# Attention maxima of the second layer: the causal mask moved from VectorE's reduction to a TensorE product, and small pieces joined in pairs

## The reference, cut to what matters

```python
# 32 heads of 16, S = 1024
scores = einsum('bqhd,bkhd->bhqk', q, k) * scale
bias = slopes[:, None, None] * rel                # rel = key position - query position
causal = rel <= 0
scores = where(causal, scores + bias, -inf)
probs = softmax(scores, axis=-1)
attn = einsum('bhqk,bkhd->bqhd', probs, v)
```

## Time and profile before

| | us |
|---|---|
| median of 3 runs (lowest, highest) | 1939.48 (1938.72, 1940.89) |
| the profiled execution | 1937.06 |
| its span, first to last instruction | 1935.3 |
| TensorE (PE) busy in it | 1842.5 |
| VectorE (DVE) busy | 1137.5 |
| ScalarE (ACT) busy | 475.4 |
| GpSimd (POOL) busy | 986.4 |
| mean granted TensorE clock, share of full speed | 0.974 |

### The profile page before, as it was taken

One profiled execution on the slowest core, in us unless ns is written; L12 is line 12 of the kernel. 1 busy time (PEld: TensorE's weight loads), 2 busy tenths in 40 slices (PEclk: granted clock), 3 DMA queues, 4 the chain that ended last, 5 costly groups with the idle time before them and its releaser, 6 DMA issues. The chain is left out here.

```text
span 1935.3 us, 27511 instructions
## 1 busy us (share of the span) xinstructions
PE 1842.5 (95%) x10157; PEld 1445.1 (75%) x10157; DVE 1137.5 (59%) x1939; ACT 475.4 (25%) x623; POOL 986.4 (51%) x1148
## 2 busy tenths in 40 slices
PE   6999999999999999999999789998889999988998
PEld 5888888888888888888888568886654444357887
DVE  6674674874856747748747733304676888535601
ACT  4221111221211212112112120002414666633200
POOL 5676755755846657557535455444711121235432
PEclk9999999999999999999999899998987999899999
DMA  2111111111111111111101122202043333011112
GB/s 95 46 55 57 45 42 46 43 50 40 43 41 46 49 41 43 39 42 49 49 14 54 44 67 82 68 22 73 3 80 52 56 54 54 2 34 46 48 49 71
DMA packets 50501, 93.57 MB, mean 48 GB/s; under 512 B 8752, under 2 KB 13488, under 8 KB 50032
## 3 DMA queue, kind: packets, MB, share of 16 engines
q1 hardware_dynamic: 49776, 91.13, 17.3%
q10 hardware_dynamic: 640, 1.31, 0.4%
HBM read 76.15 MB, written 2.10 MB: 40 GB/s over the span
## 5 line engine op out<-in xcount | busy, mean ns | idle before, releaser
L366 POOL TENSOR_TENSOR a_w_l<-a_raw,a_w_h 128x1024 fp32r<-128x1024 f32 x96 | 205.6, 2141 | 8.0
L711 DVE TENSOR_TENSOR x<-x,a_ps 128x1024 f32<-128x1024 f32 x64 | 78.0, 1219 | 167.9 <-PE a_ps L165 167.9
L1596 ACT ACTIVATE a_pr<-a_ps 128x1024 f32<-128x1024 f32 (+1 forms) x192 | 153.3, 812 | 90.2 <-PE a_ps L1803 73.2
L1546 POOL TENSOR_SCALAR_AFFINE_SELECT a_pr<-a_pr 128x256 f32<-128x256 f32 x128 | 52.0, 406 | 217.0 <-ACT a_pr L1596 215.3
L1823 PE MATMUL a_ps<-a_K,a_Q 64*128 64x512 f32 (+2 forms) x384 | 136.5, 448 | 11.5 <-DVE a_mx L1702 8.8
L165 PE MATMUL a_ps<-a_tt_h,a_w_l 128*128 128x512 f32 x376 | 147.1, 391 | 0.0
L164 PE MATMUL a_ps<-a_tt_l,a_w_h 128*128 128x512 f32 x376 | 146.6, 390 | 0.0
L163 PE MATMUL a_ps<-a_tt_h,a_w_h 128*128 128x512 f32 x376 | 146.5, 390 | 0.0
L72 POOL TENSOR_TENSOR tick<-neg_half 128x1 f32<-128x1 f32 x120 | 35.0, 292 | 215.2 <-PE a_ps L165 208.1
L1698 DVE CUSTOM_DVE_ANT_0 a_masked<-a_ps,a_mask 128x384 bf16<-128x384 f32 (+3 forms) x256 | 115.0, 486 | 32.5 <-PE a_ps L1823 31.2
L1823 PEld LDWEIGHTS a_ps<-a_K,a_Q 64*128 64x128 f32 x384 | 66.7, 198 | 84.7 <-DVE a_mx L1702 33.4
(11 more groups left out here) (247 smaller groups left out, 4727.7 us busy)
## 6 DMA issues: line engine op xcount, KB each, us to landing
a_raw<-in_a_wpair SPq DMA_DIRECT2D x96, 256.0 KB, 2.7
f_raw<-in_f_w SPq DMA_DIRECT2D x33, 320.0 KB, 2.9
a_raw_s<-in_a_wout SPq DMA_DIRECT2D x32, 256.0 KB, 3.2
f_raw<-in_f_w SPq DMA_DIRECT2D x32, 256.0 KB, 2.6
a_raw_s<-in_a_wv SPq DMA_DIRECT2D x28, 256.0 KB, 2.6
a_cst<-in_a_cst SPq DMA_DIRECT2D x32, 129.0 KB
a_Q<-a_q_h SPq DMA_DIRECT2D x64, 64.0 KB
a_K<-a_k_h SPq DMA_DIRECT2D x54, 64.0 KB
```

Source lines behind the costliest of these rows:

```text
L366: nc.gpsimd.tensor_tensor(to_l, src, to_h, ALU.subtract).then_inc(s(done), 1)
L711: nc.vector.tensor_tensor(a, a, units[i], ALU.add).then_inc(s("out_added"), 1)
L1546: nc.gpsimd.affine_select(tri, tri, [[0, 2], [1, P]], ALU.is_ge, 0.0, base=0, channel_multiplier=-1).then_inc(s("selected"), 1)
L1596: nc.scalar.activation(pr[n % SLOTS][:, 2 * i:2 * i + 2, 0:width], S[at % 2][:, :, skip:skip + width], ACT.Exp, scale=0.25).then_inc(s("sc ...
```

## The change

Each diagonal piece now gets its mask from TensorE: right behind the product of a piece stands a second, bf16 product with `laterb` and `identb` into the 128 columns of its diagonal block (128 stationary rows, 128 columns). VectorE takes every piece with a plain maximum. The pieces of 128 keys of tiles 0 and 4 of a head go into the two halves of one bank and are taken by one instruction that gives two maxima; so do those of 256 keys of tiles 1 and 5. A head thus has 10 items in place of 12. The tiles `mask` and `masked` and the load of the mask are gone, and ScalarE makes `identb` and `laterb` before it issues the first loads of `K0` to `K2`, not after. `AHEAD`, the places of the outputs between the pieces and the places of the V projections beside pair 0 are set anew for 20 items.

```diff
-PIECES = [(4, 0, BANK, False), (0, 0, P, True), (5, 0, BANK, False), (4, 1, P, True),
+PIECES = [(((4, 0),), BANK, False), (((0, 0), (4, 1)), P, True), (((5, 0),), BANK, False),
...
-AHEAD = 8
-V_AT = {2 + 3 * i: (AFTER + i // KT, i % KT) for i in range(2 * KT)}
+AHEAD, MIDDLE, BEHIND = 6, 12, 6
+V_AT = {2 + 5 * i // 2: (AFTER + i // KT, i % KT) for i in range(2 * KT)}
...
+            nc.scalar.copy(identb[:, :], ident[:, :]).then_inc(s("later_ready"), 1)
+            act.wait_ge(s("later_in"), 16)
+            nc.scalar.copy(laterb[:, :], later[:, :]).then_inc(s("later_ready"), 1)
             stack(act, 0, 0, (1,))
             stack(act, 1, 0)
             stack(act, 2, 0)
-            nc.scalar.copy(identb[:, :], ident[:, :]).then_inc(s("later_ready"), 1)
-            act.wait_ge(s("later_in"), 16)
-            nc.scalar.copy(laterb[:, :], later[:, :]).then_inc(s("later_ready"), 1)
...
-                to = mx2[p % 2][:, h, t, c:c + 1]
-                if diagonal:
-                    nc.vector.tensor_tensor_reduce(
-                        out=masked[:, at % 3, 0:width], in0=M[at % 3][:, 0:width], in1=mask[:, BANK - width:],
-                        scale=-1.0, scalar=BIG, op0=ALU.add, op1=ALU.min, accum_out=to).then_inc(s("max_taken"), 1)
+                first, last = [2 * t + c for t, c in (tiles[0], tiles[-1])]
+                to = mx2[p % 2][:, h, :, :].rearrange("p t c -> p (t c)")[:, first:last + 1:max(last - first, 1)]
+                if len(tiles) == 2:
+                    blocks = M[at % 3].rearrange("p (i q) -> p i q", i=2)
+                    nc.vector.tensor_reduce(to, blocks[:, :, 0:width], AX.X, ALU.max, negate=True
+                                            ).then_inc(s("max_taken"), 1)
                 else:
                     nc.vector.tensor_reduce(to, M[at % 3][:, 0:width], AX.X, ALU.max, negate=True
                                             ).then_inc(s("max_taken"), 1)
...
-                nc.tensor.matmul(out[:, 0:w], QT[p % SETS][rows, t * P:(t + 1) * P],
-                                 KTs[p % SETS][rows, c * BANK:c * BANK + w], start=True, stop=True
-                                 ).then_inc(s("max_made"), 1)
+                for i, (t, c) in enumerate(tiles):
+                    last = nc.tensor.matmul(out[:, i * w:(i + 1) * w], QT[p % SETS][rows, t * P:(t + 1) * P],
+                                            KTs[p % SETS][rows, c * BANK:c * BANK + w], start=True,
+                                            stop=not diagonal)
+                    if diagonal:
+                        if (p, k, i) == (0, 2, 0):
+                            pe.wait_ge(s("later_ready"), 2)
+                        last = nc.tensor.matmul(out[:, i * w + width - P:i * w + width], laterb[:, :], identb[:, :],
+                                                start=False, stop=True)
+                last.then_inc(s("max_made"), 1)
```

More of the change, by code:

```diff
@@ L1291 @@
 NS = len(STEPS)
-PIECES = [(4, 0, BANK, False), (0, 0, P, True), (5, 0, BANK, False), (4, 1, P, True),
-          (6, 0, BANK, False), (1, 0, 2 * P, True), (7, 0, BANK, False), (5, 1, 2 * P, True),
-          (3, 0, BANK, True), (2, 0, 3 * P, True), (7, 1, BANK, True), (6, 1, 3 * P, True)]
+PIECES = [(((4, 0),), BANK, False), (((0, 0), (4, 1)), P, True), (((5, 0),), BANK, False),
+          (((6, 0),), BANK, False), (((1, 0), (5, 1)), 2 * P, True), (((7, 0),), BANK, False),
+          (((3, 0),), BANK, True), (((2, 0),), 3 * P, True), (((7, 1),), BANK, True), (((6, 1),), 3 * P, True)]
 PIECES = [(h, *piece) for piece in PIECES for h in range(2)]
 NP = len(PIECES)
-AHEAD = 8
-V_AT = {2 + 3 * i: (AFTER + i // KT, i % KT) for i in range(2 * KT)}
+AHEAD, MIDDLE, BEHIND = 6, 12, 6
+V_AT = {2 + 5 * i // 2: (AFTER + i // KT, i % KT) for i in range(2 * KT)}
 def units(m):
@@ L1326, in counted @@
         p, q = 2 * g + 2, 2 * g + 3
-        pieces(p, AHEAD, 16)
+        pieces(p, AHEAD, MIDDLE)
         if g:
             count("out", g - 1, 1)
-        pieces(p, 16, NP)
+        pieces(p, MIDDLE, NP)
         pieces(q, 0, 2)
@@ L1333, in counted @@
             count("row", p)
-        pieces(q, 2, 8)
+        pieces(q, 2, BEHIND)
         count("out", g, 0)
-        pieces(q, 8, NP)
+        pieces(q, BEHIND, NP)
         pieces(q + 1, 0, 2)
@@ L1354, in paced @@
     last = MAX_AT[(2 * g + 4, AHEAD)] if g < QUADS - 2 else MAX_AT[("row", 2 * g + 3)] + 1
-    worth = [PIECES[i[1]][3] + 70 if isinstance(i[0], int) else 350 for i in items[first:last]]
+    worth = [len(PIECES[i[1]][1]) * PIECES[i[1]][2] + 70 if isinstance(i[0], int) else 350 for i in items[first:last]]
     length = sum(2 * n + 100 for _, _, n in STEPS) * 2
@@ L1392, in attention1_heads @@
         slopes = sb("kslope", [P, T], F32R), sb("qslope", [P, T], F32R)
-        mask = sb("mask", [P, BANK])
         later = sb("later", [P, P])
@@ L1412, in attention1_heads @@
         osb = [sb(f"osb{i}", [P, BANK]) for i in range(2)]
-        masked = sb("masked", [P, 3, BANK], BF16)
         KTs, QT = [(on_raw + on_cl + on_xh)[i::2] for i in range(2)]
@@ L1476, in _ @@
                         sp.dma_start(raw_slopes[i], a["a1_slopes"][i]).then_inc(qs("slopes_in"), 16)
-                    sp.dma_start(mask[:, :], a["a1_mask"]).then_inc(s("mask_in"), 16)
                     sp.dma_start(later[:, :], a["a1_later"]).then_inc(s("later_in"), 16)
@@ L1689, in maximum @@
                 at = MAX_AT[(p, k)]
-                h, t, c, width, diagonal = PIECES[k]
+                h, tiles, width, _ = PIECES[k]
                 dve.wait_ge(s("max_made"), at + 1)
@@ L1693, in maximum @@
                     dve.wait_ge(s("combined"), p - 1)
-                if k == 0 and p == 0:
-                    dve.wait_ge(s("mask_in"), 16)
-                to = mx2[p % 2][:, h, t, c:c + 1]
-                if diagonal:
-                    nc.vector.tensor_tensor_reduce(
-                        out=masked[:, at % 3, 0:width], in0=M[at % 3][:, 0:width], in1=mask[:, BANK - width:],
-                        scale=-1.0, scalar=BIG, op0=ALU.add, op1=ALU.min, accum_out=to).then_inc(s("max_taken"), 1)
+                first, last = [2 * t + c for t, c in (tiles[0], tiles[-1])]
[4 more added lines that the diff above has]
+                                            ).then_inc(s("max_taken"), 1)
                 else:
@@ L1819, in piece @@
                 out = max_bank(at)
-                h, t, c, width, _ = PIECES[k]
+                h, tiles, width, diagonal = PIECES[k]
                 rows = slice(ROWS * h, ROWS * (h + 1))
                 w = max(width, 2 * P)
-                nc.tensor.matmul(out[:, 0:w], QT[p % SETS][rows, t * P:(t + 1) * P],
-                                 KTs[p % SETS][rows, c * BANK:c * BANK + w], start=True, stop=True
-                                 ).then_inc(s("max_made"), 1)
+                for i, (t, c) in enumerate(tiles):
[8 more added lines that the diff above has]
+                last.then_inc(s("max_made"), 1)
             def max_row(p):
@@ L1875, in maxima @@
                 p, q = 2 * g + 2, 2 * g + 3
-                yield from pieces(p, AHEAD, 16)
+                yield from pieces(p, AHEAD, MIDDLE)
                 if g:
                     yield output(g - 1, 1)
-                yield from pieces(p, 16, NP)
+                yield from pieces(p, MIDDLE, NP)
                 yield from pieces(q, 0, 2)
@@ L1882, in maxima @@
                     yield max_row(p)
-                yield from pieces(q, 2, 8)
+                yield from pieces(q, 2, BEHIND)
                 yield output(g, 0)
-                yield from pieces(q, 8, NP)
+                yield from pieces(q, BEHIND, NP)
                 yield from pieces(q + 1, 0, 2)
@@ L2240, in alibi @@
     n = np.arange(P)
-    mask = np.zeros((P, BANK), np.float32)
-    mask[:, BANK - P:] = np.where(n[None, :] > n[:, None], -BIG, 0.0)
-    return {"a1_slopes": np.stack([kslope, qslope]).astype(np.float32), "a1_mask": mask,
+    return {"a1_slopes": np.stack([kslope, qslope]).astype(np.float32),
             "a1_later": np.where(n[:, None] > n[None, :], -BIG, 0.0).astype(np.float32)}
```

## The result

The changed kernel takes 2003.05 us (median of 4 runs, 1996.65 to 2006.98), against 1940.18 us of the kernel before on the same chip: a ratio of 1.0324, 95% interval 1.0304 to 1.0343. That is 63 us slower; 58 were forecast. The profiled execution took 2002.09 us, its span 2000.4.

What follows compares the result with a forecast made beforehand. PE was taken to bound the kernel, with DVE holding it up slightly. Second to seventh quads 39 us, first quad 11, pair 0 3, pair 1 5: 58 us more, 1997.5 us in all, range 1950 to 2016 us.

Steps and rivals of the forecast that it cites:

- What bounds a quad: Steady quad of 30.9 us: PE, busy 29.55 us, sets the pace; DVE holds it up by some 1.2 us.
- Rival D: Masks fit into PE's 7.7 us of weight-load waits for DVE; DVE sets the pace, 1935 us in all; chance 0.10.
- The price of a mask by rows: Steady quad: 22 masks at 0.36 us ahead of 64-row products, 10 at 0.16 ahead of values, 9.5 us.
- 0.06 us for a second product: On PE: the second mask of a pair, without a change of shape ahead of it, costs 0.06 us.
- The 0.42 us a pair: On PE: two masks side by side between scores and the next piece cost 0.42 us, mostly two changes of shape.
- The factor 0.82 and the 1.2 us of waits: Steady quad: 9.5 us scaled by 2.8 measured over 3.4 due, to 7.8, less PE's waits for DVE: 6.6 us.
- What DVE gains: DVE: unmasking saves nothing, joins 0.6 us of busy time a quad, 4.5 us over all heads; on the path nothing.
- the sum: Steady quad: 6.6 us more; whole kernel: 39 for second to seventh quads, 11 + 3 + 5 before them, 58 us.
- First quad and pairs 0 and 1: The stretch before the second quad: added masks cost 11 us in the first quad, 3 beside pair 0, 5 in pair 1.
- case A: Masks lie on PE's path, clock falls and returns as before: 1997 us, own range 1975 to 2015; chance 0.42.
- B: Masks cost the same on PE's path, but added products keep the clock up past pair 0: 1980 us; chance 0.25.
- Signs by which it was to be seen: Profile: steady quad about 37.5 us, 256 masks on one line, DVE busy about 25.5, weight loads' waits nearly gone.

Runs made afterwards that it cites:

- e2: The kernel before, its VectorE part, order and 12 items a head untouched, plus a mask product behind each of the 256 diagonal pieces: 2002.06 us, ratio 1.0316.
- e1: The changed kernel without its 256 mask products and with zero ALiBi slopes; joins, order and plain maxima stay: 1922.98 us, ratio 0.991.
- e10: The changed kernel with each mask product issued twice, one right behind the other: 2013.41 us, ratio 1.0376.
- e9: The changed kernel with the products of both heads of a pair first, then their two masks, halving the changes of shape: 1975.02 us, ratio 1.0181.
- e3: The changed kernel with masks and plain maxima, but 12 single pieces a head in the order of before, no joins: 2001.55 us, ratio 1.0327.
- e11: The changed kernel without masks or joins, 12 single pieces a head in the order of before, zero slopes: 1939.66 us, ratio 0.9998.
- e7: The kernel before with one filler product (128 rows, 512 columns) after each piece of pair 1 and of the head of pair 2: 1961.83 us, ratio 1.0114.
- e12: e6 with the first quad's score masks also made as products of 64 rows: 1924.09 us, ratio 0.9908 against the kernel before.
- e6: The changed kernel with each mask made by two products of 64 rows and 64 columns in the piece's own half of the rows: 1939.97 us, ratio 0.9993.

## Why the prediction was right, and where its terms were off

**What bounds a quad** was right: PE, with DVE behind. Rival D, that the weight loads' 7.7 us of waits were room for the masks, is refuted: e2 shows that the masks went on top, and 5.1 us of such waits stand in a quad in which PE idles 0.1 us.

**The price of a mask by rows** is what the masks cost in the changed kernel: 9.5 us a quad, 9.6 measured over e1; and 0.06 us for a second product, 0.056 in e10. The 0.42 us a pair is not confirmed by e9, whose 0.43 holds 0.16 us of idle time.

**The factor 0.82 and the 1.2 us of waits** took this to 6.6 us. That is the 6.8 of e3 over e11, the case without joins, and there both terms come out: 7.8 us of products were forecast and 7.9 measured, 1.2 us of idle time given up and 1.1 measured. The changed kernel has joins.

**What DVE gains** was mis-sized: "on the path nothing", and 0.6 us a quad of busy time where e11 and e1 differ by 1.1. Without masks the joins bring 2.2 us a quad and 17 us in all, though DVE idled 5 us of a quad; idle time on average did not mean that no hand-over was waited for. With masks in, nothing of it is left (38.2 us a quad against e3's 37.6). So the statement holds of the changed kernel and not of the step by itself, and the steady quad came out at 38.2 where 37.5 were forecast: +7.3 for +6.6. Told from the kernel without masks, the sum took 2.9 us off the rows' 9.5 and set the joins at nothing, where the runs have the full 9.6 and 2.3 of gain; that the two nearly cancel is luck.

**First quad and pairs 0 and 1**: +12.8 us for 11, +3.1 for 3, +2.0 for 5. Pair 1 was over-sized by 3.0 us, the first quad under-sized by 1.8.

**The clock** fell where case A had it, so B is refuted: the masks, which made PE busy 17.34 of 18.10 us beside pair 0, did not hold it. It came back 35 us into the first quad in place of 25, later by about the 8.8 us at which the slow part's masks were priced. What no case had is that it would fall again: in the second quad, which took 43.4 us, and for a moment in the fourth (0.73 from 1612 to 1616 us). Two windows of PE alone in the second quad of the changed kernel (length, busy, clock, DMA):

```profile
1525.00:1530.00 5.00, 5.00 (x29) 0.88 0.01 2
1530.00:1535.00 5.00, 5.00 (x20) 0.50 0.50 84
```

PE was busy without a gap where it fell. These two quads lie 5.2 and 1.5 us above the third and make up for most of the 7 us that the sum lacked of the profile's 65.1. The second quads of e2, e3 and e10, which have the masks too, ran at full clock in their profiles.

**Signs by which it was to be seen**: the steady quad, the masks' line, the 0.38 us of the first product behind a mask, ACT's longer waits (18.3 us for scores, 10.3 before) and DVE's waits (10.6 us, 6.8 more than before) came. Two did not: DVE's busy time in a quad is 26.8 us and not 25.5, and the weight loads' waits are not nearly gone.

## What to carry to other kernels

Before adding a small product to a stream of products that use a part of the array, ask what shape it has: in full-array shape it cost 0.30 us here, in the shape of its neighbours 0.06 us, and a second full-array one right behind the first 0.06 us. A mask over 128 keys can be two products of 64 rows, at the price of one more constant in SBUF. Price such a thing from a row where the same change of shape occurs, and keep the products' price apart from the idle time that they fill; and try each half of a change alone, since the joins gained 17 us that the masks had hidden.

## What was not expected of the hardware

The clock of TensorE went to half within 6 us after the last V products in twelve of the thirteen kernels profiled here, in e7 and e9 after an earlier dip beside pair 0; in e2 it fell beside pair 0, at about 1423 us. It came back at different times: at about 1474 us before, 1491 us in the changed kernel (35 us into its first quad), and 1460 us in e12, 12 us into the first quad. e12 differs from e6 by the shape and number of the first quad's 32 score masks (and one more constant), and e6 was at 0.50 until about 1483 us; its window up to 1479:

```profile
1452.70:1479.00 26.30, 25.04 (x137) 12.13 (x135) 12.23 (x21) 10.39 (x13) 3.26 (x8) 0.50 0.41 68
```

In e12 it rose behind a stretch in which PE was busy 7.57 of 9.50 us, a smaller share than in e6. That is not one execution's chance: the mean clocks are 0.978 to 0.980 in all four of e12 and 0.972 to 0.975 in all ten of e6. So the busy column does not tell whether the clock will rise. What does was not found. The rule of TensorE: Matmul & The Clock Gate in the Trainium skill (Part 1), that activity releases the throttle, does not go with the busy share of these rows.

The four timed executions of the changed kernel spread over 10 us, 0.5%, and so do 19 of the kernel before (1935.55 to 1945.26). The mean granted clocks of the four are 0.968, 0.967, 0.967 and 0.972 for 2002.09, 2006.98, 2004.01 and 1996.65 us: the fastest is the one whose clock was highest.
